# Attention stage of a four-stage block: second row maximum turned in the projections' bank, the turn of x one step sooner, factor turns in steps 0 and 6

## What is computed

```python
def _L0_attn_a_ref(x, Wq, Wk, Wv, Wo):
    q, k, v = (x @ W.T).reshape(B, S, H, dk).transpose(0, 2, 1, 3)   # for Wq, Wk, Wv
    scores = jnp.einsum('bhqd,bhkd->bhqk', q, k) / jnp.sqrt(jnp.float32(dk))
    scores = jnp.where(causal, scores, jnp.finfo(scores.dtype).min)
    probs = jax.nn.softmax(scores, axis=-1)
    attn = jnp.einsum('bhqk,bhkd->bhqd', probs, v)
    return attn.transpose(0, 2, 1, 3).reshape(B, S, D) @ Wo.T
...
x = x + _L0_attn_a_ref(_layernorm(x), Wq, Wk, Wv, Wo)
x = x + _L0_ffn_ref(_layernorm(x), gate_cp, up_cp, down_cp)
x = x + _L0_attn_b_ref(_layernorm(x), ...)
x = x + _L0_ffn_ref(_layernorm(x), gate_cp, up_cp, down_cp)
```

## Time and profile before

| | before |
|---|---|
| median of 3 runs | 840.97 us |
| the profiled execution | 838.48 us |
| its span, first to last instruction | 836.7 us |
| granted TensorE clock, mean | 0.975 |
| attention, periods 0 to 15 | about 38 to 370 us of the span |

### The profile page before, as it was taken

One profiled execution on the slowest core, in us unless ns is written; L12 is line 12 of the kernel. 1 busy time (PEld: TensorE's weight loads), 2 busy tenths in 40 slices (PEclk: granted clock), 3 DMA queues, 4 the chain that ended last, 5 costly groups with the idle time before them and its releaser, 6 DMA issues.

```text
span 836.7 us, 19306 instructions
## 1 busy us (share of the span) xinstructions
PE 772.9 (92%) x6818; PEld 658.4 (79%) x6818; DVE 626.0 (75%) x1269; ACT 493.8 (59%) x967; POOL 243.5 (29%) x321
## 2 busy tenths in 40 slices
PE   7789999999989999869999989999999879999998
PEld 7667777777767777648989888989888859988897
DVE  6678877777777778747888768689988657777765
ACT  2155555555545556566656657587977746666644
POOL 4057742222223323311001010156666461000000
PEclk9899999999999999978999999999999999999999
DMA  6866666666576655575666650000034135777741
GB/s 169 118 133 100 94 99 100 93 93 90 77 138 95 99 83 79 163 273 194 248 234 235 234 183 2 1 1 2 0 119 170 38 116 194 260 268 267 265 151 52
DMA packets 70983, 111.48 MB, mean 133 GB/s; under 512 B 7061, under 2 KB 27958, under 8 KB 70854
## 3 DMA queue, kind: packets, MB, share of 16 engines
q1 hardware_dynamic: 68848, 108.47, 49.1%
q10 hardware_dynamic: 2048, 1.88, 1.1%
HBM read 41.82 MB, written 42.81 MB: 101 GB/s over the span
## 4 chain that ended last, share of the span: by engine, by line
PE 54%; DVE 14%; issue 9%; SPq 8%; DMA 8%; ACT 7%; ACTq 0%; DVEq 0%; POOL 0%; POOLq 0%
PE bank L416 9%; PE bank L418 8%; PE bank L417 8%; PE pair_a L922 4%; DMA stk<-fx 4%; PE bank L936 3%; DVE inter L1961 3%; PE pair_b L891 3%; SPq L606 3%; SPq L489 3%; PE pair_a L1222 2%; PE pair_a L1167 2%; DMA stack<-mrow 2%; PE pair_b L1170 2%; DVE spline L2039 2%
## 5 line engine op out<-in xcount | busy, mean ns | idle before, releaser
L416 PE MATMUL bank<-wd_hi,in_hi 128*128 128x256 f32 x512 | 147.1, 287 | 1.1 <-DVE in_lo L1966 0.9
L418 PE MATMUL bank<-wd_hi,in_lo 128*128 128x256 f32 x512 | 146.3, 286 | 0.0
L417 PE MATMUL bank<-wd_lo,in_hi 128*128 128x256 f32 x512 | 146.0, 285 | 0.0
L1784 DVE TENSOR_REDUCE mx<-pair_b 128x6 f32<-128x768 f32 x124 | 118.0, 951 | 35.0 <-PE pair_b L903 34.6
L682 POOL TENSOR_SCALAR_AFFINE_SELECT prob<-prob 128x512 f32<-128x512 f32 x128 | 81.8, 639 | 208.2 <-ACT prob L1384 207.7
L1549 ACT ACTIVATE in_hi<-inter 128x512 fp32r<-128x512 f32 x128 | 80.7, 630 | 103.9 <-DVE inter L1961 97.7
L1384 ACT ACTIVATE prob<-pair_a 128x768 f32<-128x768 f32 x128 | 103.6, 809 | 61.1 <-PE pair_a L922 59.7
L1966 DVE TENSOR_TENSOR in_lo<-inter,in_hi 128x512 fp32r<-128x512 f32 x128 | 89.0, 695 | 60.9 <-ACT in_hi L1549 59.4
L416 PEld LDWEIGHTS bank<-wd_hi,in_hi 128*128 128x128 f32 x512 | 98.3, 192 | 6.3 <-DVE in_lo L1966 1.7
L417 PEld LDWEIGHTS bank<-wd_lo,in_hi 128*128 128x128 f32 x512 | 98.2, 192 | 4.8
L418 PEld LDWEIGHTS bank<-wd_hi,in_lo 128*128 128x128 f32 x512 | 98.2, 192 | 0.0
(11 more groups left out here) (233 smaller groups left out, 1955.1 us busy)
## 6 DMA issues: line engine op xcount, KB each, us to landing
stk<-fx SPq DMA_DIRECT2D x128, 252.0 KB
stack<-stage SPq DMA_DIRECT2D x184, 128.0 KB, 4.5
fx<-fs SPq DMA_DIRECT2D x32, 512.0 KB, 3.6
fx<-fs SPq DMA_DIRECT2D x32, 256.0 KB, 3.8
fx<-fs SPq DMA_DIRECT2D x16, 504.0 KB
fx<-fs SPq DMA_DIRECT2D x16, 252.0 KB
X<-in_attn_a_x SPq DMA_DIRECT2D x14, 256.0 KB, 5.7
result<-X SPq DMA_DIRECT2D x7, 512.0 KB, 7.8
```

The costliest lines, as they stand in the source:

```text
L416: pe.matmul(dst, l_hi, r_hi, start=first, stop=False)
L417: pe.matmul(dst, l_hi, r_lo, start=False, stop=False)
L418: return pe.matmul(dst, l_lo, r_hi, start=False, stop=last)
L1784: dve.tensor_reduce(mx[:, h, :, p % PR, :], src[:, :, 0:3 * P].rearrange("p n (t k) -> p n t k", t=3), AX.X, ALU.max).then_inc(a_mx, 1)
```

## The change

Five edits, which hang together. `turn_max` of h = 1 goes to `bank_p` (`max_bank`), so that `bank_t` is free in step 1; `turn_x`, `copy_xT` and `low_xT` move from step 2 to step 1, and `turn_x` waits for the split of h = 0 and not of h = 1. In step 1 `turn_max` waits for the residual that empties `bank_p`. The factor portions move from steps 0 and 1 to steps 0 and 6, the second into `bank_t`. The table's load moves from the end of period 3 to period 4, and the store of the down weights from the end of period 8 to period 9, each behind the max rows of h = 1.

```diff
-        factor_bank = (bank_y, bank_p)
+        factor_bank = (bank_y, bank_t)
+        max_bank = (bank_t, bank_p)
...  SP, period
                 max_rows(b, u, 1)
+                if b == 4:
+                    sp.wait_ge(s_c, 24)
+                    sp.dma_start(feat.rearrange("p r c -> p (r c)"), feat_in).then_inc(s_feat, 16)
+                if b == 9:
+                    store_down()
                 if nxt2:
                     stack_half(b + 2, u, 0)
...
-                if b == 3:
-                    sp.wait_ge(s_c, 24)
-                    sp.dma_start(feat.rearrange("p r c -> p (r c)"), feat_in).then_inc(s_feat, 16)
-                if b == 8:
-                    store_down()
...  TensorE, turn_max
-                    i = pe.transpose(bank_t[0:HH, P * t:P * t + P], mx2[:, h, t, :], ident[:, :])
+                    i = pe.transpose(max_bank[h][0:HH, P * t:P * t + P], mx2[:, h, t, :], ident[:, :])
...  TensorE, period
-                    if 4 <= b < 9 and p < 2:
+                    if 4 <= b < 9 and p in (0, 6):
                         if p == 0:
                             pe.wait_ge(a_at, upto(a_at, b - 1, 1))
                         else:
-                            pe.wait_ge(a_res, upto(a_res, b - 2, 1))
+                            pe.wait_ge(a_ml, upto(a_ml, b + 1, 1))
...
-                    if 4 <= b < 9 and p in (2, 3):
+                    if 4 <= b < 9 and p == 2:
...
+                    if 5 <= b < 10 and p == 1:
+                        if b < 8:
+                            pe.wait_ge(s_ce, 2 * (b - 4))
+                        else:
+                            pe.wait_ge(s_wdn, 2 * (b - 7))
                     if p == 1:
+                        pe.wait_ge(a_res, upto(a_res, b - 2, 1))
+                        turn_max(b, 1)
+                    if p == 1 and nxt2:
                         pe.wait_ge(a_ml, upto(a_ml, b, 1))
-                        turn_max(b, 1)
-                    if p == 2 and nxt2:
-                        pe.wait_ge(a_ml, upto(a_ml, b, 2))
                         turn_x(b + 2, u)
...
                             pe.wait_ge(a_xl, upto(a_xl, b + 2, 1))
-                            pe.wait_ge(a_res, upto(a_res, b - 2, 1))
+                            pe.wait_ge(a_ml, upto(a_ml, b, 2))
...  ScalarE, period
-                    if 4 <= b < 9 and p < 2:
+                    if 4 <= b < 9 and p in (0, 6):
...
-                    if p == 2 and nxt2:
+                    if p == 1 and nxt2:
                         copy_xT(b + 2, u)
...  VectorE, period
                     if p == 1:
                         split_max(b, 1)
-                    if p == 2 and nxt2:
+                    if p == 1 and nxt2:
                         low_xT(b + 2, u)
```

## The result

The changed kernel takes 830.02 us (median of 4 runs, 828.21 to 834.41) against 839.64 for the kernel before: a ratio of 0.9892, 95% interval 0.9851 to 0.9934, or 9.1 us less. Measured again on another occasion it gave 0.9869 (0.9837 to 0.9901). The forecast was 834.2, within 829.5 to 840.5, and 6.8 us less. Single executions of one kernel lie 6 us and more apart, so the time shows the whole of the change and the profile, period by period, shows its parts.

A forecast was written before the change was run, and what follows sets the result against it. TensorE, busy 92% of the span, was taken as the bound. Gains of 1.4, 1.6, 1.49, 1.98, 0.55 and -0.21 us over groups of periods gave 6.8, so 834.2 from the 840.97 median; range 829.5 to 840.5.

The forecast's parts named there:

- The shortened step: Steps 1 to 3: turn of x fills holes in step 1, so step 4 comes 0.51 + 0.17 = 0.68 us sooner.
- The second clock of step 4: Step 4 waits for max rows of h = 1, so periods loading x keep only 0.1 to 0.7 of 0.7 us.
- the first rival: Step 4: max rows end last wherever x is loaded; periods 1, 2, 3, 9, 11 lose 1.8 us: 836.0; chance 0.14.
- The factor portions: Leaving step 1 moves nothing there; in step 6 a portion costs 0.55 us in periods 4 to 6, 1.05 in 7, 8.
- The covers in step 0: The portion in step 6 absorbs max-row waits in the following step 0: 0.25 us into period 6, 0.49 into 8.
- the second rival: SP's large transfers collide elsewhere, with stage DMAs and step 0's max rows; 3.12 us given back: 837.3; chance 0.12.
- The transfers: Table and down-weights store put behind the max rows: step 4 waits of 1.34 us (period 4) and 1.78 (period 9) go.
- The third: Step 2: low half of x delays the maxima, scores of step 3 1.0 us late in 13 periods: 847.2; chance 0.07.
- The fourth: TensorE's clock: period 8 has a 1.03 us dip; without it 833.2, with two more 836.3; no separate chance.
- The fifth: Step 4 is set by the rows and factors cost what they free: within 1 us of 841; chance 0.07.
- The sum: Gains of all attention periods together: 6.8 us, giving 834.2 from the median of 840.97.
- the lower bound: 829.5: 0.3 more in periods 1, 2, 3, 9, 11, 0.7 in 10, dip gone, 3.2 in all, plus spread of medians.

The follow-up runs named there:

- the second profile: The changed kernel, unaltered, profiled again, with no stretch at the low clock in attention; ratio 0.9869 (0.9837 to 0.9901) to the kernel before.
- two experiments: Each on the changed kernel: low half of x back behind the maxima of step 2, ratio 0.9885; ScalarE's copy of x done twice in step 1, 0.9904.

## Why the prediction was right, and where its sizes were off

**The shortened step.** The mechanism was right: 0.68 to 0.7 us a period forecast, 0.62 in period 12, and putting the turn back takes 6.6 us. The term was 0.07 too large, and it was the halving of the eight transposes that was off. The push of step 2 by 0.16 us was in the sum (271.13 for 270.96), and the scores of step 2 start as forecast. But step 3 starts 0.43 us sooner and not 0.51: `turn_o`, now alone behind the scores, takes 0.59 us until step 3 starts (267.81 to 268.40), where behind the turn of x it took 0.53 of the 1.02 (`turn_o` is this line of the kernel before):

```profile
273.33 0.60 PE L949 MATMUL bank<-ident,oT 128*128 128x128 f32 x4
```

In step 3 itself 0.20 came, where 0.17 was forecast, although its scores are stretched by 0.06 by the low half in front of the maxima.

**The second clock of step 4.** Right in kind: of the six periods 1, 2, 3, 9, 10 and 11, which load x and carry no portion, four did not get the 0.6 us in the second profile (1, 3, 10 and 11), and four in the first (2, 3, 10 and 11), where period 1 can't be read for its low clock. With 1, 2, 3, 10 and 11 together 1.1 us came, where 1.6 were forecast. A period that loads x has no fixed bound: period 3 waited 0.28 us in one profile and 0.58 in another, period 2 0.30 and nothing. Rows were seen 1.7 us after the engines were done in period 10 and 1.3 in period 11; the 1.0 to 1.5 taken was a little short, and the 2.0 us of the Trainium skill (DMA: Bandwidth & Descriptors, Anatomy of one DMA) is above both. The page gives that figure for transfers issued from GpSimd, and the prediction left this out: the rows here are issued on SyncE's queue. The gain of zero, which the prediction drew from it and made the first rival, came in period 3 alone; periods 1, 2 and 11 gained 0.21, 0.64 and 0.28.

**The factor portions.** This term was mis-sized. In step 6 a turned portion costs 0.26 to 0.29 us, not 0.55, and eight matmuls 0.93, not 1.05. The step that failed is that the portion was counted "on TensorE's path in full". Its own time is 0.49 us and it makes `turn_o` behind it 0.06 shorter, so step 6 grows by 0.43 us; and step 7 shrinks by 0.14, half of it before its scores, which without a portion are stretched (by the maxima of step 6, as the order of the code suggests). For the eight matmuls it is 1.09 us of their own and 0.15 less in step 7. That a portion out of step 1 moves nothing there was right, as the put-back turn shows.

**The covers in step 0.** The waits of 0.25 and 0.49 are gone as forecast. Not all of it is the portion's doing: the one of 0.25 is also gone with the transfers alone moved. Without the second portion waits of 0.22 and 1.20 us stand in step 0 of periods 5 and 8. The table, too, delays the rows of step 0, as the second rival had it: 0.86 us of waiting with the transfers alone, 0.22 once x is turned sooner as well, 0.21 with the portion but x turned late, none with both.

**The transfers.** For all of periods 4 and 9, 1.49 and 1.98 were forecast and 1.85 and 2.48 measured. Both waits are gone, as forecast. Period 9 does not wait for rows at all, although it loads x. That the portion in step 6 of period 8 gives SP and the DMA engines some 0.9 us of lead is a reading, not shown; without the portion 0.35 us of waiting come back.

**Rivals.** The first holds for part of its periods. The second holds for the table alone. The third was excluded by two experiments: the slack in front of the low half is 0.3 us, and only what exceeds it is paid. The fourth has the dip of period 8 too small: 1.03 us came from comparing it with period 7, which ends in the wait of 0.49; step by step it is 1.52. The fifth fell.

**The sum.** Too small by 0.9 us against the traces, +0.4 in period 4, +0.5 in 9, +0.5 in 5 and 6, +0.2 in 7 and 8, -0.5 in 1, 2, 3 and 11, -0.2 in 12 and 13. The time says 9.1 us with an interval of 5.5 to 12.5, so the 1.4 us between attention's gain and the time's lie within the interval. That 830.0 lies inside the range is in part luck: the kernel before came out 1.3 us lower in this comparison, at 839.64, and the gains counted into the lower bound reach only 831.0, the rest of it being allowed for spread.

## What to carry to other kernels

Work put in front of a wait is cheaper than its duration, and work put in a gapless step can still find a hole one step on, as the portion of 0.49 us here, which cost 0.29: look at the next two steps before it is charged in full. When a step is made ready sooner, look which transfer it reads, and what stands before that transfer in the queue; a bulk load that nobody needs soon belongs behind the few small rows that the next step waits for. Parts of such a change don't add, so each is to be tried both alone on the old kernel and taken out of the new one.

## What was not expected of the hardware

TensorE's clock. The same wait of 1.62 us stands in step 0 of period 1 in all 14 profiles of this study within 0.12; in six of them a stretch at 1.2 GHz follows, in eight none. It lasts between 3 and 10 us and begins near the end of the wait or up to 1.5 us behind it. The changed kernel was profiled twice, once with it and once without: period 1 took 21.92 and 19.80 us, so here it cost 2.1 us. In this profile it began during the wait, in which TensorE stood still, and ended in step 2:

```profile
59.00:60.00 1.00, 0.53 (x4) 0.54 (x6) 0.97 (x2) 0.00 (x0) 1.00 (x2) 0.64 0.14 51
60.00:61.00 1.00, 1.00 (x16) 0.71 (x16) 0.35 (x3) 0.70 (x1) 0.22 (x1) 0.50 0.68 197
...
66.00:67.00 1.00, 1.00 (x24) 0.55 (x20) 1.00 (x2) 0.70 (x1) 0.26 (x2) 0.95 1.03 170
```

This is larger than most of the effects of this study, and explains part of the spread between runs of one kernel; comparing periods without it, step by step, resolved tenths of a microsecond, where the times leave an interval of some 3 us to either side. What starts it is not shown: period 8 of the kernel before has such a stretch behind a wait of 0.49 us, and with the turn of x put back it comes in the same step without a wait.
